# Decoder layer on one core: the softmax maxima turned in f32 and split into halves afterwards, the low half made from PSUM

## What is computed

```python
kqv = x @ Wqkv + bqkv                       # reshaped to (b, s, 3, 16, 32)
scores = jnp.einsum('bsnh,btnh->bnst', k, q) / math.sqrt(HEAD_SIZE)
scores = jnp.triu(scores) + -10000.0 * jnp.tril(ones, k=-1)
attn = jax.nn.softmax(scores, axis=2)
out = jnp.einsum('bnkq,bknh->bqnh', attn, v)
```

## Time and profile before

| | |
|---|---|
| median of 3 runs | 706.75 us (705.85 to 708.07) |
| the profiled execution, its time | 705.09 us |
| its span | 703.4 us |
| TensorE busy | 665.6 us (95% of the span), 4290 matmuls |
| VectorE busy | 520.8 us (74%), 1220 instructions |
| ScalarE busy | 494.4 us (70%) |
| GpSimd busy | 400.7 us (57%) |
| DMA | 54.33 MB, mean 77 GB/s |

### The profile page before, as it was taken

How to read it: one execution, slowest core, us unless ns; L and a number is a source line. 1 busy time by engine, 2 the same in 40 slices (tenths; PEclk the granted TensorE clock), 3 DMA queues, 4 the chain that set the end, 5 groups by cost and what they waited for, 6 DMA issues and landing times. The chain is left out here.

```text
span 703.4 us, 12518 instructions
## 1 busy us (share of the span) xinstructions
PE 665.6 (95%) x4290; PEld 377.2 (54%) x4290; DVE 520.8 (74%) x1220; ACT 494.4 (70%) x1141; POOL 400.7 (57%) x508
## 2 busy tenths in 40 slices
PE   8879999998998999799989999999999999999996
PEld 3434554454444455455444454545545887578845
DVE  4776767978989889989756669947779795486644
ACT  5789889888898789888887863466745755166620
POOL 6036246765999934874686377966794234113331
PEclk9999999999999999999999999999999999999999
DMA  7888754612333126451341001010000000010001
GB/s 240 229 240 228 182 145 130 181 51 58 118 105 87 58 86 165 121 119 41 57 73 61 1 0 61 16 46 0 1 2 30 32 1 2 1 61 1 1 16 46
DMA packets 45023, 54.33 MB, mean 77 GB/s; under 512 B 5920, under 2 KB 33824, under 8 KB 44960
## 3 DMA queue, kind: packets, MB, share of 16 engines
q1 hardware_dynamic: 41264, 46.85, 22.1%
q0 software_dynamic: 3264, 6.29, 5.5%
q10 hardware_dynamic: 432, 0.39, 0.2%
HBM read 45.00 MB, written 12.71 MB: 82 GB/s over the span
## 5 line engine op out<-in xcount | busy, mean ns | idle before, releaser
L1528 DVE CUSTOM_DVE_ANT_0 ee<-psb,mask,clip 128x512 f32<-128x512 f32 (+3 forms) x256 | 131.5, 542 | 23.2 <-PE psb L1037 22.2
L1276 ACT ACTIVATE ee<-ee,nm 128x512 f32<-128x512 f32 (+3 forms) x256 | 142.1, 559 | 1.6 <-DVE nm L1528 1.6
L1936 POOL TENSOR_TENSOR hl<-ring,hh 128x512 f16<-128x512 f32 x64 | 80.5, 1270 | 90.2 <-ACT hh L1412 65.6
L1286 ACT ACTIVATE ee<-psb 128x512 f32<-128x512 f32 (+1 forms) x192 | 95.5, 521 | 26.4 <-PE psb L1054 19.4
L1866 POOL TENSOR_SCALAR_AFFINE_SELECT ee<-ee 128x256 f32<-128x256 f32 x128 | 55.9, 452 | 66.9 <-ACT ee L1286 66.5
L1182 PE MATMUL psb<-wd,hl 128*128 128x512 f16 x240 | 91.0, 379 | 1.4 <-POOL hl L1936 1.4
L1180 PE MATMUL psb<-wd,hh 128*128 128x512 f16 x240 | 91.0, 379 | 0.0
L1037 PE MATMUL psb<-ks,qs 128*128 128x512 f16 (+3 forms) x256 | 73.1, 303 | 12.9 <-DVE nm L1528 5.9
L1054 PE MATMUL psb<-qs,ks 128*128 128x384 f16 (+3 forms) x256 | 61.0, 304 | 8.6 <-ACT ee L1286 5.6
L1883 POOL TENSOR_TENSOR rs<-ve,half 128x1 f32<-128x1 f32 (+1 forms) x24 | 20.6, 859 | 72.9 <-DVE ve L1597 72.7
L994 PE MATMUL psb<-xh,wqk 128*128 128x512 f16 x240 | 59.9, 379 | 0.4 <-ACT wqk L1253 0.4
(11 more groups left out here) (217 smaller groups left out, 1673.1 us busy)
## 6 DMA issues: line engine op xcount, KB each, us to landing
qs<-parts SPq DMA_DIRECT2D x48, 128.0 KB, 2.7
ks<-parts SPq DMA_DIRECT2D x45, 128.0 KB, 2.9
parts<-qhl SPq DMA_DIRECT2D x16, 256.0 KB, 2.3
parts<-khl SPq DMA_DIRECT2D x16, 256.0 KB, 2.2
x<-in_x SPq DMA_DIRECT2D x4, 1024.0 KB, 7.5
ct<-in_ctxT SPq DMA_DIRECT2D x4, 1024.0 KB, 5.2
out<-x SPq DMA_DIRECT2D x16, 256.0 KB, 2.0
xt<-in_xT SPq DMA_DIRECT2D x14, 256.0 KB, 3.3
```

The costliest lines, as they stand in the source:

```text
L1276: e.activation(dst, dst, ACT.Exp, bias=NM[:, n % 4, col:col + 1], scale=-1.0, accum_out=DEN[:, n % 4, col:col + 1]).then_inc(sem("exp"), 1)
L1286: e.activation(ET[H % ET_SLOTS][:, base:base + width], PSB[:, bank["turn", H, item], 0:width], ACT.Exp, scale=SC).then_inc(sem("et"), 1)
L1528: e.tensor_tensor_reduce(E[H % E_SLOTS][:, EOFF[i]:EOFF[i] + w], PSB[:, bank["score", H, i], 0:w], MASK[:, S - w:S], -SC, CLIP[:, i:i + 1] ...
L1936: e.tensor_tensor(HS[it][1][:], pair(b, it // 2)[:, it % 2, :] if b in SEVEN else ring(b, it)[1], HS[it][0][:], ALU.subtract).then_inc(sem ...
```

## The change

- Step 1 is gone, with its table `MQ_AT`, the tile `MHL`, the f16 identity (and the GpSimd instruction that made it, L1970).
- TensorE turns `NM` itself, 128x16 f32, with `e.transpose` against the f32 identity: 16x128 f32 in PSUM. It waits for the last `weigh` of the group.
- ScalarE makes the high half of that with the scale `-M_UNIT`: 16x128 f16.
- A new VectorE step, `shift_low` ("mlow"), makes the low half from PSUM and the high half: 16x128 f16. It is put in the list with `late(0)`, at the next slot's start, and `mput` behind it.
- `MROW` is [16, 2, 128]; the DMA to DRAM reads it as 16 partitions of two rows. It waits for mlow in place of mrow.
- The bank of "mt" is emptied by mlow, not by mrow.

```diff
-WAIT = {'high': 1, 'low': 1, ...
+WAIT = {'mlow': 0, 'high': 1, 'low': 1, ...
...
-    "mt": lambda n: ("mrow", n),
+    "mt": lambda n: ("mlow", n),
...
         add("mt", n)
         add("mrow", n)
-        add("mput", n)
+        late(WAIT["mlow"], lambda: (add("mlow", n), add("mput", n)))
...
-        shift.setdefault(MQ_AT[n], []).append(lambda n=n: add("mq", n))
...
-    IDENT16 = sb(ctx, "ident16", [P, P], F16)
-    MHL, MROW = sb(ctx, "mhl", [P, 2, 32], F16), sb(ctx, "mrow", [32, P], F16)
+    MROW = sb(ctx, "mrow", [16, 2, P], F16)
...
         def shift_rows(n):
             emptied(("mt", n))
-            pe.wait_ge(*by_shift(n))
-            pe.wait_ge(*by_made("ident16"))
-            e.matmul(PSB[0:32, bank["mt", n], 0:P], MHL[:, n % 2, :], IDENT16[:], start=True,
-                     stop=True).then_inc(sem("mt"), 1)
+            pe.wait_ge(*by("weigh", 4 * n + 3, 0))
+            pe.wait_ge(*by_consts())
+            e.transpose(PSB[0:16, bank["mt", n], 0:P], NM[:, n % 4, :], IDENT[:]).then_inc(sem("mt"), 1)
...
-            e.activation(MROW[:], PSB[0:32, bank["mt", n], 0:P], ACT.Copy).then_inc(sem("mrow"), 1)
+            e.activation(MROW[:, 0, :], PSB[0:16, bank["mt", n], 0:P], ACT.Copy, scale=-M_UNIT).then_inc(sem("mrow"), 1)
...
-        def shift(n):
-            high, low = MHL[:, n % 2, 0:16], MHL[:, n % 2, 16:32]
-            dve.wait_ge(*by("weigh", 4 * n + 3, 0))
-            if n >= 2:
-                dve.wait_ge(*by("mt", n - 2))
-            e.tensor_scalar(high, NM[:, n % 4, :], -M_UNIT, None, ALU.mult).then_inc(sem("mq"), 1)
-            dve.wait_ge(*by_shift(n, False))
-            e.scalar_tensor_tensor(out=low, in0=NM[:, n % 4, :], scalar=-M_UNIT, in1=high, op0=ALU.mult,
-                                   op1=ALU.subtract).then_inc(sem("mq"), 1)
+        def shift_low(n):
+            dve.wait_ge(*by("mrow", n))
+            e.scalar_tensor_tensor(out=MROW[:, 1, :], in0=PSB[0:16, bank["mt", n], 0:P], scalar=-M_UNIT, in1=MROW[:, 0, :],
+                                   op0=ALU.mult, op1=ALU.subtract).then_inc(sem("mlow"), 1)
...
         def put_shifts(n):
-            sp.wait_ge(*by("mrow", n))
-            e.dma_start(MSCR[n].rearrange("k h (i t) -> (k h i) t", i=T), MROW[:]).then_inc(sem("mput"), 16)
+            sp.wait_ge(*by("mlow", n))
+            e.dma_start(MSCR[n].rearrange("k h (i t) -> (h i) k t", i=T), MROW[:]).then_inc(sem("mput"), 16)
             sp.wait_ge(*by_mput(n))
```

More of the change, by code:

```diff
@@ L86 @@
     253, 14: 263, 15: 273}
-MQ_AT = {0: 12, 1: 28, 2: 44, 3: 60, 4: 76, 5: 92, 6: 109, 7: 126, 8: 141, 9: 156, 10: 174, 11: 188, 12: 207, 13: 221,
-    14: 236, 15: 253}
 MT_AT = {0: 13, 1: 29, 2: 46, 3: 61, 4: 77, 5: 93, 6: 109, 7: 127, 8: 143, 9: 159, 10: 175, 11: 189, 12: 209, 13: 222,
@@ L92 @@
     236}
-WAIT = {'high': 1, 'low': 1, 'vtake': 2, 'r1': 2, 'norm': 6, 'exp': 4, 'eb': 0, 't1': 1, 't3': 1, 'oh': 2, 'ol': 2,
+WAIT = {'mlow': 0, 'high': 1, 'low': 1, 'vtake': 2, 'r1': 2, 'norm': 6, 'exp': 4, 'eb': 0, 't1': 1, 't3': 1, 'oh': 2, 'ol': 2,
     'ek': 1, 'scan_q': 2, 'scan_p': 25, 'seed': 6, 'refine': 8, 'divide': 14, 'r2': 1, 'x2h': 0, 'x2l': 0, 'expand':
@@ L820, in by_made @@
     def by_made(what):
-        return sem("made"), {"nt": 1, "zp": 2, "rows": 4, "ident16": 5, "half": 6, "edge": 8}[what]
-    def by_shift(n, low=True):
-        return sem("mq"), 2 * n + 1 + low
+        return sem("made"), {"nt": 1, "zp": 2, "rows": 4, "half": 5, "edge": 7}[what]
     def by_turned(n):
@@ L1747, in _ @@
                 expand(*a)
-            elif name == "mq":
-                shift(*a)
+            elif name == "mlow":
+                shift_low(*a)
             elif name == "t1":
@@ L1967, in _ @@
                     e.tensor_tensor(X[b][:, t, :], X[b][:, t, :], BO[:], ALU.add).then_inc(sem("xb"), 1)
-            elif name == "mq" and a[0] == 0:
-                pool.wait_ge(*by_consts())
-                e.tensor_scalar(IDENT16[:], IDENT[:], 1.0, 0.0, ALU.mult, ALU.add).then_inc(sem("made"), 1)
             elif name == "small":
```

## The result

| | before | with the change |
|---|---|---|
| median, this series | 706.95 us (705.26 to 708.93, 9 runs) | 711.71 us (708.39 to 718.42, 9 runs) |
| ratio, 95% interval | | 1.0085, 1.0057 to 1.0113 |
| span of the profiled execution | 703.4 us | 709.6 us |

The change makes the kernel slower, by 0.0085 x 706.95 = 6.0 us (4.0 to 8.0). The forecast was 707.7, 1 us slower, in a range up to 710.8.

What follows compares the result with a forecast made beforehand. TensorE, busy 95% of the span, and its waits were taken as the bound. Terms -3.4 (step 1), +0.9 (transposes), +1.0 (group 1), +0.3 (groups 2, 5, 8), +2.1 (group 15) gave +0.9: 707.7 us from 706.75, range 704.4 to 710.8.

Steps and rivals of the forecast that it cites:

- Group 15: Last group's chain: later put and two wd loads ahead of its broadcasts cost 2.1 us, bounds 1.5 and 4.6.
- the late put: Group 15: put leaves 1.6 us later, behind mlow and L1649, so turn starts later; 1.5 us.
- the loads ahead: Group 15: two wd loads ahead delay the broadcasts; 0.6 us of group 2's 2.9, bounds 0 and 2.9.
- The first rival: Group 15's broadcasts stick behind the weight loads as at group 2: 4.6 us, not 2.1; 710.2 us; chance 0.28.
- The gains: Dropping step 1 ends the turning matmul's waits and relieves VectorE: 3.4 us saved, bounds nothing and 7.
- Groups 7 and 8: Turning matmul's waits of 0.5 and 0.37 us run into other waits; gains counted as 0.15 us and nothing.
- VectorE's relief: Scores waiting for weigh: 0.75 us gained, at group 9; a rival took 4.1 of 5.9, 704.2 us, chance 0.16.
- The f32 transposes: TensorE, 16 groups: f32 transpose at 0.11 us replaces f16 matmul at 0.054; 0.9 us added, bounds 0 and 1.8.
- The rival with 0.216: TensorE's f32 transposes take 0.216 us each: sum +2.6, 709.4 us; chance 0.06.
- mlow: New VectorE step: 0.34 us each, 5.5 in all; its waits for ScalarE's copy, up to 0.9 us, counted as nothing.
- Group 0: Put leaves 1.2 us later but lands behind a load of x anyway; counted as nothing, 1.2 us if wrong.
- Group 1: Put 1.0 us later behind weigh delays SyncE's queue, including the next stack; cost 1.0 us, bounds 0 and 1.2.

Runs made afterwards that it cites:

- e6: The change, with GpSimd's three last wd loads 11 slots later, behind group 15's broadcasts; 706.76 us, ratio 1.0005 to the kernel before.
- e7: The change, with 18 matmuls of unused result ahead of group 15's first turn, filling TensorE's stall; 709.14 us, ratio 1.0044 to the kernel before.
- e1: The change, with group 15's mlow and put right behind ScalarE's copy, the other 15 groups as in the change; 703.86 us, ratio 0.9947 to the kernel before.
- e13: The same kernel as e1, run again in a second series; 705.14 us, ratio 0.9981 to the kernel before.
- e12: e1, plus the two old step 1 VectorE instructions writing a tile nobody reads; 705.22 us, ratio 0.9980 to the kernel before.
- e14: The same kernel as e12, run again; 706.18 us, ratio 0.9999 to the kernel before.
- e8: e1, with each of the 16 f32 transposes issued five times, so 64 more; 709.65 us, ratio 1.0048 to the kernel before.
- e2: The change, with group 1's mlow and put right behind ScalarE's copy, the rest as in the change; 710.12 us, ratio 1.0045 to the kernel before.
- e3: The change, with mlow and put of groups 1 and 15 right behind ScalarE's copy; 705.09 us, ratio 0.9973 to the kernel before.
- e15: The change, with mlow and put of all 16 groups right behind ScalarE's copy; 702.83 us, ratio 0.9963 to the kernel before.
- e11: The kernel before, with only group 15's put held until VectorE step L1649 has ended; 712.36 us, ratio 1.0086 to the kernel before.

## Why the prediction was wrong

**Group 15, the step that failed.** The sum had 2.1 us for it, 1.5 for the late put and "0.6 us of the 2.9" for the loads ahead; it cost 5.7: 1.2 for the late put, 3.2 for the loads, and 1.3 for a lower clock that no term had. The mechanism, the put's 1.6 us and the broadcasts' issue at 348.4 were right; the size of the collision was not. I had also read the merged row as two loads ahead of both broadcasts, where the second load stands between them; and the upper bound of 4.6 is not 1.5 + 2.9 = 4.4, but the rival's figure. The second broadcast took 3.2 us more than without the loads (e6), a little over the 2.9 of the earlier trace rows: the smaller rows of `wd`, my reason to take a fifth, bought nothing. The first rival had this mechanism (4.6 us, 710.2 in all) and should have been the forecast. The estimate by the Trainium skill (DMA: Bandwidth & Descriptors, Queues, rings and completion order) was 0.7 us for it; the trace does not agree, 3.2 us.

**TensorE's clock, in no case.** The lag rises by another 1.3 us (4.9 to 6.2) while the clock is at 0.50 to 0.70. Filling the stall keeps it at 1.00 (e7), and over all executions the mean granted clock is lower in just the kernels with the long stall. The trace of before showed such a fall (granted clock 0.50 from 53 to 55 us, behind the 1.9 us wait at 51.26), and I did not read it. So a stall of 4 us cost 5.7.

**The rest of the sum**, without group 15's 2.1, was -1.2 us. The change's trace has +0.5 before group 15, the lag of e6's -0.8; e6 in all, with the late put but no collision, has a ratio of 1.0005. e1 and e13, which have group 15 at once and all the rest of the change, have 0.9964, so -2.5 us. The forecast of the rest lies between these figures, but partly by luck, as its parts show:

- **The gains**, 3.4 us forecast. From the lag, group 4 gave 1.3, group 6 0.35, group 7 0.7, group 8 0.6, group 9 0.8, group 10 1.0, group 12 0.8: 5.5 together. Groups 7 and 8, counted at 0.15 and 0, did give theirs. But new waits took much back: 1.1 us at 151 us, where a matmul now waits for a VectorE step (its bank has changed, as mlow empties its own later), 0.4 at `turn` of group 7, 0.9 at `turn` of group 9, whose put I had placed within its room, and 0.9 at 305 for a bank that mlow empties. I had noted that the banks move and counted nothing.
- **VectorE's relief.** Scores wait 4.5 us for `weigh` instead of 5.9, near the 5 I named; its value is likely 1 to 2 us (e12, e14), not 0.75.
- **The f32 transposes.** 0.11 us as forecast (343.26 to 343.37; e8). The rival with 0.216 falls, and with it, for these, the four passes of the Trainium skill (FP8 and Floating Point Precision, TensorE Precision Notes).
- **mlow** took 0.27 us, not 0.34, with no outlier, and its 1.4 us of waits for ScalarE's copy cost nothing that shows:

```profile
L1530 DVE SCALAR_TENSOR_TENSOR mrow<-psb,mrow 16x128 f16<-16x128 f32 x16 | 4.3, 272 | 1.5 <-ACT mrow L1285 1.4
```

- **Group 0**: its `turn` waits 0.4 us instead of 0.8; nothing, as counted.
- **Group 1**, 1.0 us forecast. The put left at 53.06, 0.8 us later, and the wait for the stack grew from 0.9 to 2.3 us, not to 1.9. In the change's lag it is 1.9 us at that point (in e6's, too), and 3.4 with a fall of the clock behind; in e2's trace it is 0.1 at that point. In time e2 gives 2.8 with 2.4 of uncertainty, e3 nothing, so what the group costs the kernel stays open. The 1.2 us that `turn` waits there was not in the sum: I had followed the put into SyncE's queue and not to its own group.

So small terms were off by a microsecond or two in both directions and cancelled, which is luck; one term was off by 3.6 and decided.

## What to carry to other kernels

- When a DMA on which TensorE waits next is moved past a bulk load in another queue, charge it with the longest delay that such a collision shows in the trace, and put the load elsewhere before anything else is tuned. Here moving three loads by 11 slots took away 4.5 us of group 15's 5.7, by the traces. But look at what the load meets at its new place: there it cost 0.9 us again.
- The last link of a pipeline has no next group to catch up in. Work put back by "one slot" costs little at fifteen places together (0 to 1.3 us in e13 against e15, within the noise) and all of the loss at the sixteenth: decide such a delay for each item, not by a rule.
- A stall of TensorE can cost more than its length, here 5.7 us where the delay alone was 4.4. Look in the trace of before for what followed its longest stalls.

## What the runs showed of the hardware

**A fall of the clock stands behind stalls, but not behind all.** In the thirteen traces, read from 20 to 80, 280 to 310 and 335 to 365 us, every fall of the granted clock to 0.50 begins during a wait of TensorE of 0.9 us or more, or up to 2.6 us behind one, and lasts 3 to 7 us. (One more in the attention, in e12 at 216 us, stands behind several shorter waits, 0.5, 0.8 and 0.2 us.) But the same wait has one in one execution and none in another: the 2.40 us at 299.77 in the kernel before had none, the 2.26 us at 300.30 in e11 had one, from 301 to 305; the change's 1.85 us at 51.13 had none, the 1.89 us at 51.26 before had one. All three traces with a wait of 3.7 us or more (the change, e2, e11) had one with it. A part of the scatter of single executions, up to 10 us within a kernel, goes with this: in the change the execution of 708.4 us has a mean granted clock of 0.995, that of 718.4 us one of 0.983, and in all kernels the slower executions tend to have the lower one. Whether the clock makes them slow or goes with a longer wait, no run tests. In e2 the clock was still low when the stall had ended, and stayed so for nearly 5 us (the matmuls resume at 351.9):

```profile
348.00:350.00 2.00, 0.00 (x0) 0.00 (x0) 0.69 (x1) 0.40 (x1) 2.00 (x4) 0.93 1.14 177
350.00:352.00 2.00, 0.11 (x1) 0.14 (x2) 0.00 (x0) 0.00 (x0) 0.60 (x1) 0.50 1.24 222
352.00:354.00 2.00, 2.00 (x7) 0.94 (x6) 0.00 (x0) 0.98 (x2) 0.40 (x1) 0.50 1.10 159
354.00:356.00 2.00, 2.00 (x8) 1.20 (x7) 0.00 (x0) 0.72 (x1) 0.00 (x0) 0.50 1.23 204
356.00:358.00 2.00, 2.00 (x10) 0.84 (x9) 1.09 (x2) 1.99 (x4) 0.10 (x1) 0.86 0.18 31
```

**A small DMA issued behind another queue's bulk load lands late, and of two the second can suffer more**: 2.9 and 5.5 us to landing in the change, 3.0 and 5.5 in e2, 3.0 and 5.6 in e7, 2.0 and 4.9 in e11, but 5.0 and 5.3 at group 2 of the kernel before; 2.2 and 2.3 in e6 without the loads. In the change, e2 and e7 the second lands 0.2 to 0.4 us behind the first load of `wd` (354.20 and 353.98 in the change), in e11 0.6 us ahead of it. Why is open.
